# Taking the last pair of chunks of a gated RWKV scan one chunk at a time, with a small part of the last residual on VectorE

## The chip, the cores and the metric

One core of a Trainium2 chip runs the whole program. The metric is device time in microseconds (us), the median over several executions; lower is better. TensorE (PE in the profile) does matrix products into PSUM, VectorE (DVE) and ScalarE (ACT) work on SBUF and PSUM, GpSimd (POOL) works on SBUF only, and SyncE (SP) issues the transfers of this kernel (ACT issues one).

## The reference

The input x has 32 sequences of 128 tokens and 256 channels, in float32. Two residual blocks follow each other:

```python
def _birwkv(r, k, v, w, u):
    ew, ek = jnp.exp(w.reshape(-1)), jnp.exp(k)
    Af, Bf = _wkv_scan(ek, v, ew)                    # forward scan
    Ab, Bb = _wkv_scan(ek[:, ::-1], v[:, ::-1], ew)  # backward scan
    cur = jnp.exp(u.reshape(-1) + k)
    wkv = (Af + Ab[:, ::-1] + cur * v) / (Bf + Bb[:, ::-1] + cur)
    return jax.nn.sigmoid(r) * wkv

x = x + jnp.tanh(g_xattn[0]) * _birwkv(_layernorm(x), ctx, ctx, w, u)
x = x + jnp.tanh(g_ffn[0]) * _L0_ffn_ref(_layernorm(x), ...)
```

The second block quantises its input, the weights (256 to 704 and back) and the hidden values to 8-bit steps. The step of the input comes from the largest absolute value of the whole normalised tensor, so nothing of that block's products can start before all 32 sequences have been normalised.

## The kernel before

**Layout.** Tokens lie on the 128 partitions. `x_all` holds x for all sequences, 256 channels each, and is updated in place. The two scans of a channel are one product with a 128x128 matrix of decay weights, so numerator and denominator of a channel for all 32 sequences come from one matmul.

**The scan stage.** The 256 channels are worked through in 32 chunks of 8 channels, and the chunks in 16 pairs (`PAIRS`, index m; chunk j = 2m or 2m + 1). One chunk is 8 x 32 = 256 values in a partition. For a chunk, `accumulate(j)` on TensorE makes 16 matmul pieces (line 909) and gives `ab_done`; `denominator(j)` on VectorE (line 706) multiplies the denominator with 1 + exp(-normalised x) and gives `den_done`; `reciprocal(m)` on ScalarE takes both chunks of a pair at once, a Ln (line 493) and an Exp (line 496) of 512 values, since exp(-ln d) is 1/d, and gives `rden_done`; `mix(j)` on VectorE (line 715) multiplies the numerator with it and gives `mix_done`; `residual(m)` on GpSimd (line 397) adds both chunks of a pair into `x_all` and gives `x1_done`.

**Order around the last pairs.** Each engine runs its own queue in the written order. VectorE does the denominator of a chunk of the next pair ahead of each mix; after pairs 10 to 15 it also runs `early_stats` (line 679), the statistics of the first 128 channels, for six sequences at a time (two after the last pair). ScalarE runs one more weight copy (`keep_weights(2)`), a change of its function table and a tanh after the last reciprocal.

**The normalisation stage.** For eight groups of four sequences, `late_stats(g)` on VectorE waits for all of `x1_done`, takes the statistics of the second 128 channels (line 679) and merges both halves (line 695); `rstd2(g)` on GpSimd is four small operations (lines 365 to 371); `normalise(g)` on ScalarE (line 504) does three sequences of the group and `normalise_last(g)` on GpSimd (line 421) the fourth; `turn_z(g)` on TensorE transposes the result (line 933), `keep_z(g)` on ScalarE copies it out of PSUM (line 511), and `peak_z(g)` on VectorE finds the largest value (line 722). GpSimd runs `rstd2(0)`, then `rstd2(g + 1)` and `normalise_last(g)` in turn. VectorE runs `late_stats` of groups 0 to 2 and then alternates `peak_z(g - 3)` and `late_stats(g)`. From group 3 on TensorE adds five idle products of 512 columns behind each group (`idle_wide`, line 956). ScalarE alternates `normalise(g)` and `keep_z(g - 1)`. Then follow the global peak, the gate and up products (line 1002), the down products (line 1035) and the output.

Of the kernel before, what the change touches and what calls it, by code (L numbers as in the profile page):

```python
# [22 lines left out]
ALU = mybir.AluOpType  # L23
# [17 lines left out]
def gated_rwkv_ffn(nc, x, ctx_kv, g_xattn, g_ffn, w, u, clip_x, clip_down, w_gate, w_up, w_down, out):  # L41
    SEQS, T, C = x.shape
# [22 lines left out]
    BANKS = 6  # L65
    HALF = CK * SEQS
    assert T == P and IR == P // 2 and UNIT == 512 and CH == 2 and 2 * HALF == 512 and CG == 2

    with ExitStack() as stack:
# [111 lines left out]
        def group(tile, g):  # L181
# [34 lines left out]

            "ctx_back", "ek_done", "pk_done", "ab_done", "den_done", "ln_done", "rden_done", "mix_done", "x1_done",

# [112 lines left out]
        def _(pool):  # L331
# [61 lines left out]
            def residual(m):  # L393
# [4 lines left out]
                                        ALU.add).then_inc(s["x1_done"], 1)  # L398

            for g in range(GROUPS):  # L400
                rstd1(g)
# [7 lines left out]
            own_weights(0)  # L409
            for m in range(PAIRS):  # L410
                residual(m)
                j = 2 * (m + 1) + 6
                if j in MADE:
                    add_own(MADE.index(j))
                    if j != MADE[-1]:
                        own_weights(MADE.index(j) + 1)
            def normalise_last(g):

                n = g * GS + GS - 1
                pool.wait_ge(s["sc2_done"], g + 1)  # L420
                nc.gpsimd.tensor_scalar(z_all[:, n * C:(n + 1) * C], x_all[:, n * C:(n + 1) * C], rs2[:, n:n + 1],  # L421
                                        mr2[:, n:n + 1], ALU.mult, ALU.add).then_inc(s["z_last"], 1)
# [34 lines left out]
        def _(act):  # L457
# [31 lines left out]
            def reciprocal(m):  # L489

                act.wait_ge(s["den_done"], 2 * m + 2)
                wait(act, s["rden_done"], m)
                nc.scalar.activation(lnd, den[:, m % 2, :], ACT.Ln).then_inc(s["ln_done"], 1)  # L493
                act.wait_ge(s["ln_done"], m + 1)
                wait(act, s["mix_done"], 2 * m - 2)
                nc.scalar.activation(rden[:, m % 2, :], lnd, ACT.Exp, scale=-1.0).then_inc(s["rden_done"], 1)  # L496

            def normalise(g):
# [79 lines left out]

            for m in range(PAIRS):
                reciprocal(m)  # L580
# [8 lines left out]
                if m == 12:  # L589
                    exp_clips()  # L590
            keep_weights(2)
            tanh_ffn()
# [48 lines left out]
        def _(dve):  # L641
# [45 lines left out]
            def late_stats(g):  # L687

                dve.wait_ge(s["x1_done"], PAIRS)
                for i in range(GS):  # L690
# [19 lines left out]
            def mix(j):  # L710
                m, i = j // 2, j % 2
                dve.wait_ge(s["rden_done"], m + 1)
                if i == 0:
                    wait(dve, s["x1_done"], m - 1)
                nc.vector.scalar_tensor_tensor(mixed[:, m % 2, i * CK:(i + 1) * CK, :], half_bank(j, 1), S["tanh_x"],  # L715
                                               rden[:, m % 2, i * HALF:(i + 1) * HALF].rearrange("p (c b) -> p c b", b=SEQS),
                                               ALU.mult, ALU.mult).then_inc(s["mix_done"], 1)

            def peak_z(g):
# [34 lines left out]
            done = 0  # L754
            for m in range(PAIRS):
                if m + 1 < PAIRS:
                    denominator(2 * m + 2)
                mix(2 * m)
                if m + 1 < PAIRS:
                    denominator(2 * m + 3)  # L760
                mix(2 * m + 1)
# [10 lines left out]
                if m > 9:  # L772
                    n = min(6, SEQS - done)
                    early_stats(done, n)
                    done += n
            assert done == SEQS
            for g in range(GROUPS):
                if g >= 3:
                    peak_z(g - 3)
                late_stats(g)  # L780
            for g in range(GROUPS - 3, GROUPS):
                peak_z(g)
# [283 lines left out]
```

## Time and profile before

| what | value |
|---|---|
| device time, median of 3 runs | 218.35 us (218.22 to 220.37) |
| the profiled execution, its own time | 217.56 us |
| its span in the profile | 215.6 us |
| busy share of the span: PE, DVE, ACT, POOL | 79%, 79%, 72%, 64% |
| granted TensorE clock, mean | 0.93 of full |

No engine is busy throughout: the program is a row of stages with a different limit in each. The change touches the seam between two of them, from about 96 us to about 108 us of the span, where the scan stage ends and the second normalisation begins. What counts there is the order in which things wait for each other, and the chain of waits and the timelines of the single engines show that; the busy shares do not.

### The profile page before, as it was taken

What the parts mean: (1) busy time and instruction counts of PE and PEld (TensorE: products, weight loads), DVE (VectorE), ACT (ScalarE), POOL (GpSimd) and SP (SyncE); (2) the same over time, 40 slices, a digit from 0 to 9 for tenths busy, and PEclk for the clock granted to TensorE, in tenths of its full rate; (3) what the DMA queues carried; (4) which work ended last, traced back from release to release, by engine and by line L of the source; (5) the groups of instructions that cost most, each with busy time, mean ns of one, the idle gap of its engine ahead of it and who ended that gap; (6) DMA issues with size and microseconds to landing.
All of it is one profiled execution on the core that took longest, in us unless ns stands there. A gap on an engine that the chain in (4) does not pass through costs nothing.

```text
span 215.6 us, 3369 instructions
## 1 busy us (share of the span) xinstructions
PE 169.9 (79%) x1121; PEld 122.7 (57%) x1126; DVE 170.5 (79%) x345; ACT 155.7 (72%) x235; POOL 137.4 (64%) x157
## 2 busy tenths in 40 slices
PE   4599977959899999972078888599799924989950
PEld 4456527959899999962056553234243403756620
DVE  0769495537657689997689679997999998999992
ACT  3459698573996996996479978578798844899400
POOL 3364223469399999884688807749887750039991
PEclk9969999999999999999556999999999995899995
DMA  3999999999999996300000000000000000004458
GB/s 98 341 371 348 348 319 292 287 292 298 289 320 252 267 243 177 101 0 2 0 0 0 0 3 2 0 0 0 3 0 0 0 0 0 3 0 146 167 195 273
DMA packets 43327, 29.30 MB, mean 136 GB/s; under 512 B 2224, under 2 KB 43056, under 8 KB 43312
## 3 DMA queue, kind: packets, MB, share of 16 engines
q1 hardware_dynamic: 43168, 28.84, 46.7%
q10 hardware_dynamic: 144, 0.26, 0.3%
q8 instruction: 9, 0.15, 0.3%
q14 instruction: 6, 0.05, 0.1%
HBM read 24.65 MB, written 4.46 MB: 135 GB/s over the span
## 4 chain that ended last, share of the span: by engine, by line
PE 36%; DVE 25%; ACT 14%; DMA 9%; issue 7%; POOL 3%; SPq 1%; DVEq 1%; ACTq 0%
PE ps L909 10%; PE ps L1002 9%; PE ps L1035 8%; DMA hidden<-lag_w 6%; PE ps L893 5%; DVE hidden L799 4%; DMA hidden<-in_ctx 3%; ACT hidden L504 3%; DVE h_space L856 2%; DVE hidden L817 2%; PE ps L940 2%; DVE h_peaks L828 2%; ACT silu_out L623 2%; ACT hidden L575 2%; DVE bn L679 2%
## 5 line engine op out<-in xcount | busy, mean ns | idle before, releaser
L909 PE MATMUL ps<-hidden 128*128 128x128 f32 (+1 forms) x512 | 58.7, 276 | 6.3 <-DMA hidden<-lag_w 3.0
L909 PEld LDWEIGHTS ps<-hidden 128*128 128x128 f32 x512 | 57.8, 192 | 7.6 <-issue 3.3
L397 POOL TENSOR_TENSOR x_all<-x_all,silu_out 128x512 f32<-128x512 f32 x16 | 24.3, 1526 | 8.2 <-DVE silu_out L715 8.2
L828 DVE TENSOR_REDUCE h_peaks<-hidden (+2 forms) x24 | 26.0, 1123 | 2.0 <-POOL hidden L440 1.3
L1035 PE MATMUL ps<-wdT,z_t 128*128 128x256 bf16 (+1 forms) x192 | 25.0, 285 | 2.9 <-ACT z_t L637 2.9
L706 DVE SCALAR_TENSOR_TENSOR h_space<-z_t,ps 128x256 f32<-128x256 f32 x32 | 18.9, 595 | 8.9 <-PE ps L909 8.7
L637 ACT ACTIVATE z_t<-h_space 128x1024 bf16<-128x1024 int8 (+3 forms) x12 | 20.1, 1754 | 6.8 <-DVE h_space L856 6.8
L1035 PEld LDWEIGHTS ps<-wdT,z_t 128*128 128x128 bf16 (+1 forms) x192 | 17.0, 101 | 10.8 <-issue 4.8
L623 ACT ACTIVATE silu_out<-ps,mix_scale 128x1024 f32<-128x1024 f32 (+1 forms) x18 | 18.3, 1019 | 5.8 <-PE ps L1002 3.4
L933 PE MATMUL ps<-ident,hidden 128*128 128x128 f32 x64 | 11.6, 342 | 12.6 <-POOL hidden L421 11.1
L453 POOL TENSOR_TENSOR x_all<-x_all,z_t 128x512 f32<-128x512 f32 x6 | 10.7, 1802 | 15.5 <-DVE z_t L874 15.5
L715 DVE SCALAR_TENSOR_TENSOR silu_out<-ps,small,silu_out 128x256 f32<-128x256 f32 x32 | 15.2, 477 | 5.7 <-ACT silu_out L496 4.8
L485 ACT ACTIVATE z_t<-x_all,mr,nr 128x256 f32<-128x256 f32 x32 | 16.4, 589 | 3.6 <-POOL mr L359 3.6
L893 PE MATMUL ps<-hidden,flip 128*128 128x512 f32 x32 | 16.1, 646 | 2.8 <-DMA hidden<-in_ctx 2.8
L933 PEld LDWEIGHTS ps<-ident,hidden 128*128 128x128 f32 x64 | 9.6, 179 | 15.4 <-ACT hidden L504 14.5
L440 POOL TENSOR_TENSOR hidden<-silu_out,up_out 128x1024 f32<-128x1024 f32 x6 | 14.5, 2410 | 5.5 <-ACT up_out L627 5.4
L671 DVE BATCH_NORM_STATS2 bn<-x_all 128x6 f32<-128x256 f32 x32 | 11.2, 414 | 8.1 <-DMA x_all<-in_x 7.9
L440 POOL TENSOR_TENSOR hidden<-h_space 128x1024 f32<-128x1024 f32 x6 | 14.4, 2401 | 4.8 <-ACT h_space L627 4.8
L493 ACT ACTIVATE up_out<-h_space 128x512 f32<-128x512 f32 x16 | 10.0, 624 | 10.3 <-DVE h_space L706 10.3
L856 DVE TENSOR_SCALAR h_space<-hidden,small 128x1024 int8<-128x1024 f32 (+3 forms) x12 | 15.2, 1334 | 0.1
L504 ACT ACTIVATE hidden<-x_all,mr,rs 128x256 f32<-128x256 f32 x24 | 12.6, 594 | 3.3 <-POOL mr L371 3.3
L354 POOL TENSOR_TENSOR ve<-mv,consts 128x4 f32<-128x4 f32 x8 | 1.6, 199 | 20.5 <-DVE mv L675 20.5
(105 smaller groups left out, 357.2 us busy)
## 6 DMA issues: line engine op xcount, KB each, us to landing
hidden<-lag_w SPq DMA_DIRECT2D x26, 512.0 KB, 7.3
x_all<-in_x SPq DMA_DIRECT2D x8, 512.0 KB, 8.8
hidden<-in_ctx SPq DMA_DIRECT2D x8, 512.0 KB, 9.0
out<-x_all SPq DMA_DIRECT2D x16, 256.0 KB, 2.4
xq<-in_L_ffn_w_down SPq DMA_DIRECT2D x1, 704.0 KB, 5.9
xq<-in_L_ffn_w_gate SPq DMA_DIRECT2D x1, 640.0 KB, 6.9
h_space<-in_L_ffn_w_up SPq DMA_DIRECT2D x1, 640.0 KB, 6.0
lag_w<-up_out ACTq DMA_DIRECT2D x1, 255.0 KB, 7.2
```

Of the source, the lines that this page charges most:

```text
L397: nc.gpsimd.tensor_tensor(xs, xs, mixed[:, m % 2, :, :].rearrange("p c b -> p b c"), ALU.add).then_inc(s["x1_done"], 1)
L440: nc.gpsimd.tensor_tensor(hidden[:, b * HB + k * BT:b * HB + (k + 1) * BT], silu_even[n % 2], up_even[n % 2], ALU.mult).then_inc(s["h_even ...
L504: last = nc.scalar.activation(z_all[:, n * C:(n + 1) * C], xs[:, i, :], ACT.Identity, scale=rs2[:, n:n + 1], bias=mr2[:, n:n + 1])
L623: nc.scalar.activation(silu_out[:, 1, 0:cols] if k % 2 else silu_even[even % 2], banks[0], ACT.Silu, scale=mix_scale[:, 0, k:k + 1]).then_ ...
L637: nc.scalar.activation(hq[:, b % 2, cols], h8[:, b % 2, cols], ACT.Copy).then_inc(s["hq_done"], 1)
L828: nc.vector.tensor_reduce(h_peaks[:, bass.ds(KA * b + k, 1)], hidden[:, bass.ds(b * HB + k * BT, cols)], AX.X, ALU.max, apply_absolute_val ...
L856: nc.vector.tensor_scalar(h8[:, b % 2, k * BT:last], hidden[:, b * HB + k * BT:b * HB + last], S["inv_h"], None, ALU.mult).then_inc(s["h8_ ...
L893: last = nc.tensor.matmul(turned(g)[:, half], flip[:, :], ring[g % SLOTS][:, half], start=True, stop=True)
L909: last = nc.tensor.matmul(ps[:, j % BANKS, c * 2 * SEQS:end * 2 * SEQS], lag_tile(j)[:, c, :], ekp[:, (j * CK + c) * 2 * SEQS:(j * CK + en ...
L933: last = nc.tensor.transpose(ps[:, z_bank(g) + h, i * T:(i + 1) * T], z_all[:, n * C + h * P:n * C + (h + 1) * P], ident[:, :])
L1002: last = nc.tensor.matmul(dst, wT[:, h, k * P:k * P + rows_], whole_x(b)[:, j, h, :], start=(h == 0), stop=(h == CH - 1))
L1035: last = nc.tensor.matmul(ps[:, 4 * sl + i, j * C:(j + 1) * C], lhs, rhs, start=(k == 0 and j == 0), stop=(k == KA - 1), skip_group_check= ...
```

## The change

- The last pair (chunks 30 and 31) is taken chunk by chunk on ScalarE: a Ln and an Exp of 256 values for each chunk (`reciprocal_half`), with semaphores of their own.
- On VectorE the last steps are put in another order: both mixes of pair 14 stand ahead of the denominator of chunk 31; the mix of chunk 30 stands ahead of it too. The eight early statistics that are left are spread: one, then five, then the last two behind the late statistics of group 0.
- The residual of the last pair is split in three. GpSimd adds chunk 30 for all sequences and chunk 31 for sequences 8 to 31 (`residual_half`); VectorE adds chunk 31 for sequences 0 to 7 (`residual_own`).
- The late statistics of groups 0 and 1 wait for the residual of chunk 30 and for VectorE's own part; those of the later groups wait for everything on GpSimd (each group also behind VectorE's own part by order).

```diff
@@ gpsimd @@
+            def residual_half(j, first):
+
+                pool.wait_ge(s["mix_done"], j + 1)
+                xs = x_all[:, :].rearrange("p (b c) -> p b c", c=C)[:, first:SEQS, j * CK:(j + 1) * CK]
+                part = mixed[:, j // 2 % 2, j % 2 * CK:(j % 2 + 1) * CK, first:SEQS]
+                nc.gpsimd.tensor_tensor(xs, xs, part.rearrange("p c b -> p b c"), ALU.add).then_inc(s["x1_done"], 1)
...
-            for m in range(PAIRS):
+            for m in range(PAIRS - 1):
                 residual(m)
...
+            residual_half(CHUNKS - 2, 0)
+            residual_half(CHUNKS - 1, OWN_SEQS)
@@ scalar @@
+            def reciprocal_half(j):
+
+                m, i = j // 2, j % 2
+                cols = slice(i * HALF, (i + 1) * HALF)
+                act.wait_ge(s["den_done"], j + 1)
+                act.wait_ge(s["rden_done"], m)
+                nc.scalar.activation(lnd[:, cols], den[:, m % 2, cols], ACT.Ln).then_inc(s["ln_half"], 1)
+                act.wait_ge(s["ln_half"], i + 1)
+                act.wait_ge(s["mix_done"], 2 * m - 2)
+                nc.scalar.activation(rden[:, m % 2, cols], lnd[:, cols], ACT.Exp, scale=-1.0).then_inc(s["rden_half"], 1)
...
-            for m in range(PAIRS):
+            for m in range(PAIRS - 1):
                 reciprocal(m)
...
+            for j in (CHUNKS - 2, CHUNKS - 1):
+                reciprocal_half(j)
             keep_weights(2)
@@ vector @@
             def late_stats(g):
 
-                dve.wait_ge(s["x1_done"], PAIRS)
+                if (g + 1) * GS <= OWN_SEQS:
+                    dve.wait_ge(s["x1_done"], PAIRS)
+                    dve.wait_ge(s["x1_own"], 1)
+                else:
+                    dve.wait_ge(s["x1_done"], PAIRS + 1)
...
-                dve.wait_ge(s["rden_done"], m + 1)
+                if m < PAIRS - 1:
+                    dve.wait_ge(s["rden_done"], m + 1)
+                else:
+                    dve.wait_ge(s["rden_half"], i + 1)
...
+            def residual_own():
+
+                j = CHUNKS - 1
+                dve.wait_ge(s["mix_done"], CHUNKS)
+                xs = x_all[:, :].rearrange("p (b c) -> p b c", c=C)[:, 0:OWN_SEQS, j * CK:(j + 1) * CK]
+                part = mixed[:, j // 2 % 2, j % 2 * CK:(j % 2 + 1) * CK, 0:OWN_SEQS]
+                nc.vector.tensor_tensor(xs, xs, part.rearrange("p c b -> p b c"), ALU.add).then_inc(s["x1_own"], 1)
...
+            denominator(CHUNKS - 2)
+            mix(CHUNKS - 4)
+            mix(CHUNKS - 3)
+            early_stats(done, 1)
+            mix(CHUNKS - 2)
+            denominator(CHUNKS - 1)
+            early_stats(done + 1, 5)
+            mix(CHUNKS - 1)
+            residual_own()
             for g in range(GROUPS):
                 if g >= 3:
                     peak_z(g - 3)
                 late_stats(g)
+                if g == 0:
+                    early_stats(SEQS - 2, 2)
```

VectorE's queue before the change, from the denominator of chunk 30 to the first merge of the second normalisation. L706 is the denominator, L715 the mix, L679 the statistics, L695 the merge; `h_space` holds the denominators, `silu_out` the mixed values and the reciprocals:

```order
L706 SCALAR_TENSOR_TENSOR h_space<-z_t,ps 128x256 [waits ln_done,ab_done]
L715 SCALAR_TENSOR_TENSOR silu_out<-ps,small,silu_out 128x256 [waits x1_done,rden_done]
L706 SCALAR_TENSOR_TENSOR h_space<-z_t,ps 128x256 [waits ab_done]
L715 SCALAR_TENSOR_TENSOR silu_out<-ps,small,silu_out 128x256 [waits rden_done]
L679 BN_STATS bn<-x_all 128x6 [waits x1_done]
L679 BN_STATS bn<-x_all 128x6 x5
L715 SCALAR_TENSOR_TENSOR silu_out<-ps,small,silu_out 128x256 [waits x1_done,rden_done]
L715 SCALAR_TENSOR_TENSOR silu_out<-ps,small,silu_out 128x256 [waits rden_done]
L679 BN_STATS bn<-x_all 128x6 [waits x1_done]
L679 BN_STATS bn<-x_all 128x6
L679 BN_STATS bn<-x_all 128x6 [waits x1_done]
L679 BN_STATS bn<-x_all 128x6 x3
```

The same stretch of VectorE's queue after the change (L735 is now the denominator, L747 the mix, L704 the statistics, L757 VectorE's own part of the residual):

```order
L735 SCALAR_TENSOR_TENSOR h_space<-z_t,ps 128x256 [waits ln_done,ab_done]
L747 SCALAR_TENSOR_TENSOR silu_out<-ps,small,silu_out 128x256 [waits x1_done,rden_done]
L747 SCALAR_TENSOR_TENSOR silu_out<-ps,small,silu_out 128x256 [waits rden_done]
L704 BN_STATS bn<-x_all 128x6 [waits x1_done]
L747 SCALAR_TENSOR_TENSOR silu_out<-ps,small,silu_out 128x256 [waits x1_done,rden_half]
L735 SCALAR_TENSOR_TENSOR h_space<-z_t,ps 128x256 [waits ab_done]
L704 BN_STATS bn<-x_all 128x6 [waits x1_done]
L704 BN_STATS bn<-x_all 128x6 x4
L747 SCALAR_TENSOR_TENSOR silu_out<-ps,small,silu_out 128x256 [waits rden_half]
L757 TENSOR_TENSOR x_all<-x_all,silu_out 128x8x8 [waits mix_done]
L704 BN_STATS bn<-x_all 128x6 [waits x1_own,x1_done]
L704 BN_STATS bn<-x_all 128x6 x3
```

The denominator of chunk 31 has moved behind three mixes, only the mix of chunk 31 is left behind it, and an addition of 8 x 8 values stands between that mix and the late statistics.

GpSimd's queue at the same place, before (L397 is the residual, L365 the first operation of `rstd2(0)`):

```order
L397 TENSOR_TENSOR x_all<-x_all,silu_out 128x32x16 [waits mix_done] x4
L365 TENSOR_TENSOR ve<-mv,consts 128x4 [waits mv2_done]
L367 TENSOR_TENSOR rs<-ve,consts 128x4 [waits ve2_done]
L369 TENSOR_TENSOR nr<-rs,consts 128x4 [waits rs2_done]
L371 TENSOR_TENSOR mr<-nr,mv 128x4 [waits rs2_done]
```

and after:

```order
L399 TENSOR_TENSOR x_all<-x_all,silu_out 128x32x16 [waits mix_done] x3
L407 TENSOR_TENSOR x_all<-x_all,silu_out 128x32x8 [waits mix_done]
L407 TENSOR_TENSOR x_all<-x_all,silu_out 128x24x8 [waits mix_done]
L367 TENSOR_TENSOR ve<-mv,consts 128x4 [waits mv2_done]
L369 TENSOR_TENSOR rs<-ve,consts 128x4 [waits ve2_done]
L371 TENSOR_TENSOR nr<-rs,consts 128x4 [waits rs2_done]
L373 TENSOR_TENSOR mr<-nr,mv 128x4 [waits rs2_done]
```

The last addition of 512 values has become one of 256 and one of 192.

## Rows read from the trace of the kernel before

**Rows 1.** The chain of waits, at the seam: start us, length us, what.

```profile
100.67 0.79 DVE silu_out L715 x2
...
101.53 1.50 POOL x_all L397
...
103.05 0.88 DVE bn L679 x4
...
113.81 1.96 PE ps L933 x8
...
115.79 1.02 ACT z_t L511
...
118.28 0.91 ACT z_t L511
```

**Rows 2.** Timeline of DVE: start, length, line, operation [idle before <- releaser].

```profile
96.38 0.59 DVE L706 SCALAR_TENSOR_TENSOR h_space<-z_t,ps 128x256 f32<-128x256 f32 x1
97.02 0.48 DVE L715 SCALAR_TENSOR_TENSOR silu_out<-ps,small,silu_out 128x256 f32<-128x256 f32 x1
98.53 0.58 DVE L706 SCALAR_TENSOR_TENSOR h_space<-z_t,ps 128x256 f32<-128x256 f32 x1 [1.02 <-PE ps L909]
99.03 0.48 DVE L715 SCALAR_TENSOR_TENSOR silu_out<-ps,small,silu_out 128x256 f32<-128x256 f32 x1
99.42 1.25 DVE L679 BATCH_NORM_STATS2 bn<-x_all 128x6 f32<-128x128 f32 x6
100.58 0.86 DVE L715 SCALAR_TENSOR_TENSOR silu_out<-ps,small,silu_out 128x256 f32<-128x256 f32 x2
...
103.05 0.87 DVE L679 BATCH_NORM_STATS2 bn<-x_all 128x6 f32<-128x128 f32 x4 [1.21 <-POOL x_all L397]
```

**Rows 3.** Timeline of DVE further on: the merge of group 1, the first peak.

```profile
105.15 0.42 DVE L695 BATCH_NORM_AGGREGATE mv<-bn 128x2 f32<-128x12 f32 x4
...
108.75 1.22 DVE L722 TENSOR_REDUCE peaks<-hidden 128x1 f32<-128x1024 f32 x1 [1.98 <-POOL hidden L421]
```

**Rows 4.** Timeline of ACT: two Exp of 512, the first operation of the normalisation.

```profile
96.36 0.63 ACT L496 ACTIVATE silu_out<-up_out 128x512 f32<-128x512 f32 x1
...
99.81 0.63 ACT L496 ACTIVATE silu_out<-up_out 128x512 f32<-128x512 f32 x1
...
106.35 1.58 ACT L504 ACTIVATE hidden<-x_all,mr,rs 128x256 f32<-128x256 f32 x3 [3.06 <-POOL mr L371]
```

**Rows 5.** Timeline of POOL: residual of pair 14, first operations of groups 0 and 1.

```profile
99.58 1.50 POOL L397 TENSOR_TENSOR x_all<-x_all,silu_out 128x512 f32<-128x512 f32 x1 [3.46 <-DVE silu_out L715]
...
104.46 0.20 POOL L365 TENSOR_TENSOR ve<-mv,consts 128x4 f32<-128x4 f32 x1 [1.45 <-DVE mv L695]
...
106.27 0.20 POOL L365 TENSOR_TENSOR ve<-mv,consts 128x4 f32<-128x4 f32 x1
```

**Rows 6.** Groups by line and shape: busy us, mean ns | idle before, releaser.

```profile
L564 ACT ACTIVATE xq<-xq 128x256 f32<-128x256 f32 x1 | 0.4, 401 | 0.0
...
L751 DVE TENSOR_SCALAR down_row<-down_row 128x128 f32<-128x128 f32 x1 | 0.2, 227 | 4.1 <-ACT down_row L562 4.1
...
L861 DVE TENSOR_TENSOR small<-small 128x1 f32<-128x1 f32 x1 | 0.2, 157 | 0.0
```

**Rows 7.** Timeline of all engines from 79 us: a DVE operation beside a POOL residual.

```profile
79.21 3.02 POOL L397 TENSOR_TENSOR x_all<-x_all,silu_out 128x512 f32<-128x512 f32 x2
...
80.90 2.65 DVE L735 TENSOR_SCALAR down_diag<-ident,small 128x128 f32<-128x128 f32 x2
```

**Rows 8.** By stretch: PE, PEld, DVE, ACT, POOL busy (count), PEclk, DMA share, GB/s.

```profile
103.50:104.00 0.50, 0.00 (x0) 0.00 (x0) 0.47 (x4) 0.00 (x0) 0.00 (x0) 0.50 0.00 0
...
117.50:118.00 0.50, 0.45 (x4) 0.26 (x3) 0.50 (x4) 0.50 (x2) 0.34 (x3) 1.00 0.00 0
```

**Rows 9.** Timeline of PE: transposes, idle products and transposes at the full clock.

```profile
118.78 1.07 PE L933 MATMUL ps<-ident,hidden 128*128 128x128 f32 x8
119.68 1.24 PE L956 MATMUL ps<-wgT,ident_b 128*128 128x512 bf16 x5
```

More of the change, by code:

```diff
@@ L66, in gated_rwkv_ffn @@
     HALF = CK * SEQS
+    OWN_SEQS = 8
     assert T == P and IR == P // 2 and UNIT == 512 and CH == 2 and 2 * HALF == 512 and CG == 2
@@ L215, in gated_rwkv_ffn @@
             "w_rec", "w_quant", "w_cast", "w_turned", "w_stored",
-            "ctx_back", "ek_done", "pk_done", "ab_done", "den_done", "ln_done", "rden_done", "mix_done", "x1_done",
+            "ctx_back", "ek_done", "pk_done", "ab_done", "den_done", "ln_done", "rden_done", "ln_half", "rden_half", "mix_done", "x1_done", "x1_own",
             "bn1_done", "mv1_done", "ve1_done", "rs1_done", "sc1_done",  "ez_done",
@@ L754, in _ @@
             done = 0
-            for m in range(PAIRS):
-                if m + 1 < PAIRS:
-                    denominator(2 * m + 2)
+            for m in range(PAIRS - 2):
+                denominator(2 * m + 2)
                 mix(2 * m)
-                if m + 1 < PAIRS:
-                    denominator(2 * m + 3)
+                denominator(2 * m + 3)
                 mix(2 * m + 1)
@@ L772, in _ @@
                 if m > 9:
[L773 to L776, printed above, removed]
+                    early_stats(done, 6)
+                    done += 6
+            denominator(CHUNKS - 2)
[7 more added lines that the diff above has]
+            residual_own()
             for g in range(GROUPS):
```

## The prediction

> **What bounds the kernel now.** The busy shares say little here: the four engines lie between 64% and 79%, so the limit changes from stage to stage. I read the chain of waits first, at the seam between the scans and the second normalisation, then the timeline of each engine there.
>
> The chain of waits [rows 1] runs through the last two mixes on DVE (100.67 to 101.46), then through one residual of 1.50 us on POOL (101.53 to 103.03), then into the first late statistics on DVE (103.05). From there it goes on as statistics, small operations on POOL, transposes, and ScalarE's alternating copies and normalisations. DVE's timeline [rows 2] shows both sides of this: it stands idle for 1.21 us before 103.05, released by that POOL residual. Earlier it stands idle for 1.02 us before 98.53, released by PE, whose product for chunk 31 is done only then. So the last denominator cannot start before 98.53, and everything between 98.53 and 103.05, 4.52 us, is what this change can work on. It is made of: the denominator (0.58), Ln and Exp of 512 values on ACT (the second is the row at 99.81, 0.63, ending at 100.44) [rows 4], six early statistics that keep DVE until 100.58 [rows 2], two mixes, and the POOL residual of two chunks.
>
> **What is behind the seam.** All of the second normalisation hangs on the first late statistics. ACT stands idle for 3.06 us before its first normalisation at 106.35 [rows 4], so its work before (a weight copy, the table change, a tanh) is over at 103.29. The stage can come up to 3.06 us earlier before ACT itself refuses. PE has nothing to do between chunk 31 and the first transpose. If the first late statistics start earlier by d, the whole of the rest moves by d, unless something named below stands in the way. No transfer stands at the seam: the outputs are issued at the end.
>
> **The change, step by step.**
>
> *1. PE.* Nothing changes ahead of 98.53. The denominator of chunk 30 (96.38) and the first mix of pair 14 (97.02) stand where they stood [rows 2].
>
> *2. The order on DVE.* A mix lets the next instruction in after 0.39 us (99.03 to 99.42), a denominator after 0.50 (98.53 to 99.03), and six statistics take 1.16 of the queue (99.42 to 100.58), 0.19 each [rows 2]. So: mix 28 at 97.02 as before, mix 29 at 97.41 (before: 99.03), one statistic at 97.80, ready for mix 30 at about 98.0. This fills the 1.02 us in which DVE waited for PE.
>
> *3. ACT, chunk 30.* The Exp of pair 14 ends at 96.36 + 0.63 = 96.99 [rows 4], and the denominator of chunk 30 at 96.97 [rows 2]. An ACT operation of 256 values in SBUF with a constant scale took 401 ns, against 0.63 us for 512 [rows 4, 6]. The old pair took from 99.11 (end of the denominator) to 100.44, that is 1.33 = 2 x 0.63 + 0.07 for the handovers. A half takes 2 x 0.40 + 0.07 = 0.87. So the half for chunk 30 is done at 96.99 + 0.87 = 97.86 and mix 30 runs from 98.0; the queue is free at 98.39, 0.14 before PE releases the denominator of chunk 31. This work is hidden by the wait for PE. If a half cost as much as a whole (1.33), mix 30 would start at 98.35, the denominator would come at 98.74, and 0.2 would be lost.
>
> *4. The path.* Denominator of chunk 31 from 98.53 to 99.11; ACT's half 0.87, until 99.98; meanwhile DVE does five statistics from 99.03, 0.97 us, until 100.00. Mix 31 from 100.01 to 100.49 (0.48 [rows 2]). Before, it ended at 100.58 + 0.86 = 101.44. That is 0.95 us, from the halves on ACT (0.46), the overrun of the sixth statistic (100.58 against 100.44, 0.14) and one mix fewer (0.86 - 0.48 = 0.38), less a handover of 0.03.
>
> *5. The residual.* DVE adds 64 values itself. The trace has no such addition: from below, one value in 0.157; from above, 128 values of one source in 0.227 [rows 6]. I take 0.2. A handover on one engine or from ACT to DVE is 0.03 (96.99 to 97.02 [rows 2, 4]; half of ACT's 0.07): 100.52 to 100.72, and the late statistics of group 0 start at about 100.74. Before, the POOL residual stood there with its handovers: 103.05 - 101.44 = 1.61, now 0.25. That is 1.36.
>
> *6. The other condition.* Group 0 also waits for POOL's part of chunk 30. The residual of pair 14 can start 0.07 behind mix 29 (as 99.58 stood behind 99.51 [rows 2, 5]): 97.41 + 0.48 + 0.07 = 97.96, until 99.46. A residual of 512 values takes 1.50 and a POOL addition of 4 values 0.20 [rows 5], so 2.56 ns for a value: 256 values in 0.85, 192 in 0.68. Chunk 30 is done at about 100.33, 0.2 before DVE wants to start its own. If it took the full 1.5, it would end at 100.97 and cost 0.25 to 0.5.
>
> *7. POOL's part of chunk 31* starts 0.07 behind mix 31, at 100.56, and ends at about 101.25, or 101.45 if it has to let DVE go first. POOL is next wanted at 104.46 - 2.31 = 102.15 for group 0 [rows 5]: covered by 0.7 us. If that cover is gone, every 0.1 of it is 0.1 of the end.
>
> *8. The two statistics left over* (0.39) now stand before group 1. Its merge ended at 105.57 [rows 3]; it now ends at 105.57 - 2.31 + 0.39 = 103.65. POOL took it up at 106.27 [rows 5], which becomes 103.96: hidden by 0.3 us. Group 2 is 0.39 late too, hidden by the 1.98 us in which DVE waits before 108.75 [rows 3]. They cost nothing.
>
> *9. ACT at the other side* is wanted at 106.35 - 2.31 = 104.04 and is free at 103.29 even if it gained nothing. Covered by 0.75.
>
> **Sum.** 0.95 + 1.36 = 2.31 us, the same as 103.05 - 100.74. On the profiled execution: 217.56 - 2.31 = 215.25 (span 213.3). The median of the runs shown is 0.79 above that execution: 218.35 - 2.31 = 216.04. I forecast 216.1.
>
> **A row that speaks against it.** At 79.21 two POOL residuals begin, until 82.23. Two DVE operations of 128 values that fall into them take 2.65 us together, where one like it took 0.227 alone [rows 6, 7]: the first ends behind POOL's work, not beside it. DVE's new addition stands in just such a place. By the Trainium skill (SBUF — State Buffer, "SBUF: two separate sides") GpSimd and VectorE share a pair of ports, a VectorE operation with two SBUF inputs takes that pair, and whoever starts first holds it for its whole instruction. These rows agree with it for a VectorE operation of one input; none of them shows one with two. What decides is the order at 100.5: DVE hears of its own mix after 0.03, POOL after 0.07, so DVE should be first by 0.04 and pay nothing.
>
> **Rivals.**
>
> *A. As summed.* 2.1 to 2.5 us, 215.8 to 216.3. Chance 0.60.
>
> *B. DVE's addition is held by POOL.* Either POOL gets in first with its part of chunk 31: DVE's own is then done 0.68 later, at about 101.45, and the gain is 1.6; or POOL's half for chunk 30 does not shrink with its size and ends at 100.97, gain 1.85. For it: [rows 7], and a margin of only 0.04 and 0.2. Against it: the order of the handovers. 216.5 to 216.8. Chance 0.24.
>
> *C. Nothing is gained at the end.* The seam moves, and a wait further on takes it back, at ACT (cover 0.75), at POOL for group 1 (cover 0.3), or at PE. Against it: each has its cover in steps 7 to 9. About 217.3 to 218.4. Chance 0.11 with partial cases.
>
> *D. Slower: PE comes out of its low clock later.* The clock is at 0.5 (1.2 GHz) from 103.5, 5 us after PE fell idle, and at full (2.4 GHz) at 117.5 [rows 8]; eight transposes take 1.96 at the low level and 1.07 at the high one [rows 1, 9]. ACT's round of one group takes 118.28 - 115.79 = 2.49 [rows 1]. From group 3 PE also does five idle products a group, 1.24 at the high level [rows 9], so about 2.5 at the low: 1.96 + 2.5 = 4.5 against 2.49, 2.0 us late for each group in which the low clock lasts. From two such groups on it is 4.0 against a gain of 2.3: 220.0. Against it: PE's work is the same and only moved, and the rise came with group 3, before the first idle products. A rise that is earlier gains at most 0.25, since ACT has its normalisation to finish before 115.79 anyway. Chance 0.05.
>
> **How the numbers follow.** A change of 1% is 2.2 us, about what a measurement of this kernel can tell from none. The sum is 0.1 above that, so the verdict hangs on small things: A falls on the faster side in somewhat more than two of three cases (0.42), and a little comes from an earlier clock and from noise. Faster by over 1%: 0.45. Within 1%: 0.50 (the rest of A, B, C). Slower: 0.05 (D). The range takes in A and B, a gain larger by up to 0.8 (the median may lie nearer to the profiled execution, 0.79 below it), and part of C: 215.2 to 217.3.
>
> **What the profile after would show.** Mix 31 ends near 100.5; DVE's own addition, of about 0.2 us, follows at once; the late statistics of group 0 start at 100.7 to 100.8 with no wait for POOL; the residual of pair 14 starts at 98.0; POOL's new pieces take 0.85 and 0.68; ACT's first normalisation starts near 104.0 and still has idle time before it; the distance from the first late statistics to ACT's copy of group 3, 118.28 - 103.05 = 15.23 us before [rows 1], is the same. An own addition of 0.7 us or more would be B. A wait of DVE for POOL before group 0 would refute step 6. Five wide idle products of 2.5 us would be D. I would be wrong altogether if the denominator of chunk 31 no longer started at 98.5.

## The result: 0.7% faster, and the profile after

Over 20 runs each the changed kernel took 217.49 us (215.57 to 218.72) and the kernel before 218.65 us (217.42 to 220.53). The ratio is 0.993, with a 95% interval of 0.9907 to 0.9952, so the gain is 1.0 to 2.0 us. I had forecast 216.1 in a range of 215.2 to 217.3, so the direction was right and the median stood just above the range. The range had been laid around the median of three runs (218.35), where twenty gave 218.65; the ratio taken of 218.35 is 216.8, inside the range.

The profiled execution of the changed kernel took 216.45 us, with a span of 214.6 against 215.6. Its chain of waits at the seam (start, length, what), the counterpart of [rows 1]:

```profile
99.60 0.58 DVE h_space L735
100.18 0.97 DVE bn L704 x5
101.15 0.46 DVE silu_out L747
101.61 0.02 issue
101.63 0.28 DVE x_all L757
101.91 0.03 issue
101.94 0.02 DVEq L716
101.96 0.04 issue
102.00 0.88 DVE bn L704 x4
```

The POOL residual of 1.50 us has left the chain. From the start of the denominator of chunk 31 (L735) to the first late statistics it is now 2.40 us, where it was 4.52 [rows 2]: 2.12 us shorter. But the denominator itself starts at 99.60 and not at 98.53, 1.07 later. What releases it, PE's product for chunk 31, was not changed, and its distance from the denominator of chunk 30 is the same (2.16, and 2.15 before), so the delay arises ahead of the changed code. This is why the span is only 1.0 shorter. The prediction had named this very sign, a denominator of chunk 31 that no longer starts at 98.5, as the one by which it would be wrong altogether, and it is what the experiments have to explain.

DVE's timeline, for [rows 2] and [rows 3]:

```profile
97.44 0.59 DVE L735 SCALAR_TENSOR_TENSOR h_space<-z_t,ps 128x256 f32<-128x256 f32 x1
98.09 0.87 DVE L747 SCALAR_TENSOR_TENSOR silu_out<-ps,small,silu_out 128x256 f32<-128x256 f32 x2
98.89 0.28 DVE L704 BATCH_NORM_STATS2 bn<-x_all 128x6 f32<-128x128 f32 x1
99.08 0.47 DVE L747 SCALAR_TENSOR_TENSOR silu_out<-ps,small,silu_out 128x256 f32<-128x256 f32 x1
...
104.49 0.42 DVE L724 BATCH_NORM_AGGREGATE mv<-bn 128x2 f32<-128x12 f32 x4
...
107.69 1.22 DVE L762 TENSOR_REDUCE peaks<-hidden 128x1 f32<-128x1024 f32 x1 [1.59 <-POOL hidden L433]
```

The idle 1.02 us ahead of the last denominator is filled with mix 29, a statistic and mix 30 (mix 28 stood there before). ACT's timeline, for [rows 4]: the halves of chunk 30 and of chunk 31, and the first normalisation:

```profile
98.15 0.42 ACT L516 ACTIVATE up_out<-h_space 128x256 f32<-128x256 f32 x1
98.60 0.42 ACT L519 ACTIVATE silu_out<-up_out 128x256 f32<-128x256 f32 x1
100.22 0.42 ACT L516 ACTIVATE up_out<-h_space 128x256 f32<-128x256 f32 x1 [1.20 <-DVE h_space L735]
100.67 0.42 ACT L519 ACTIVATE silu_out<-up_out 128x256 f32<-128x256 f32 x1
...
105.30 1.58 ACT L527 ACTIVATE hidden<-x_all,mr,rs 128x256 f32<-128x256 f32 x3 [1.37 <-POOL mr L373]
```

POOL's timeline, for [rows 5]: the residual of pair 14, its two pieces of pair 15, the first operations of groups 0 and 1:

```profile
99.05 1.51 POOL L399 TENSOR_TENSOR x_all<-x_all,silu_out 128x512 f32<-128x512 f32 x1 [1.85 <-DVE silu_out L747]
100.52 0.84 POOL L407 TENSOR_TENSOR x_all<-x_all,silu_out 128x256 f32<-128x256 f32 x1
101.68 0.77 POOL L407 TENSOR_TENSOR x_all<-x_all,silu_out 128x192 f32<-128x192 f32 x1 [0.32 <-DVE silu_out L747]
103.41 0.20 POOL L367 TENSOR_TENSOR ve<-mv,consts 128x4 f32<-128x4 f32 x1 [0.97 <-DVE mv L724]
...
105.22 0.20 POOL L367 TENSOR_TENSOR ve<-mv,consts 128x4 f32<-128x4 f32 x1
```

### The profile page after: what moved, and what is told of

Read it like the earlier page. It is cut to its first block, busy times and chain, and to the rows that moved or that the text cites. A ratio compares the mean times of both kernels' runs of the same rounds, so it can differ in the third digit from the quotient of the medians.

```text
span 214.6 us, 3377 instructions
## 1 busy us (share of the span) xinstructions
PE 171.4 (80%) x1121; PEld 124.1 (58%) x1126; DVE 171.0 (80%) x346; ACT 156.1 (73%) x237; POOL 137.6 (64%) x158
## 4 chain that ended last, share of the span: by engine, by line
PE 35%; DVE 22%; ACT 15%; DMA 9%; issue 7%; SPq 6%; POOL 3%; DVEq 1%; ACTq 0%
PE ps L1050 9%; PE ps L1083 9%; PE ps L941 7%; PE ps L957 7%; DMA hidden<-lag_w 6%; DVE hidden L847 4%; DMA hidden<-in_ctx 3%; ACT hidden L527 3%; SPq L273 2%; DVE h_space L904 2%; DVE hidden L865 2%; PE ps L988 2%; DVE h_peaks L876 2%; ACT hidden L598 2%; ACT silu_out L648 2%
## 5 line engine op out<-in xcount | busy, mean ns | idle before, releaser
L957 PE MATMUL ps<-hidden 128*128 128x128 f32 (+1 forms) x512 | 60.6, 280 | 5.7 <-DVE hidden L678 2.5
L957 PEld LDWEIGHTS ps<-hidden 128*128 128x128 f32 x512 | 59.5, 196 | 7.2 <-DMA hidden<-lag_w 5.7
L735 DVE SCALAR_TENSOR_TENSOR h_space<-z_t,ps 128x256 f32<-128x256 f32 x32 | 19.0, 597 | 10.2 <-PE ps L957 10.0
L399 POOL TENSOR_TENSOR x_all<-x_all,silu_out 128x512 f32<-128x512 f32 x15 | 22.8, 1533 | 6.1 <-DVE silu_out L747 6.0
L747 DVE SCALAR_TENSOR_TENSOR silu_out<-ps,small,silu_out 128x256 f32<-128x256 f32 x32 | 15.2, 477 | 4.3 <-ACT silu_out L508 2.6
L505 ACT ACTIVATE up_out<-h_space 128x512 f32<-128x512 f32 x15 | 9.3, 623 | 9.3 <-DVE h_space L735 9.3
L598 ACT ACTIVATE hidden<-down_row,xq 128x128 f32<-128x128 f32 x48 | 14.6, 388 | 0.0
```

The costliest lines, as they stand in the source:

```text
L399: nc.gpsimd.tensor_tensor(xs, xs, mixed[:, m % 2, :, :].rearrange("p c b -> p b c"), ALU.add).then_inc(s["x1_done"], 1)
L735: nc.vector.scalar_tensor_tensor(den[:, m % 2, i * HALF:(i + 1) * HALF].rearrange("p (c b) -> p c b", b=SEQS), ez[:, :, j * CK:(j + 1) * C ...
L957: last = nc.tensor.matmul(ps[:, j % BANKS, c * 2 * SEQS:end * 2 * SEQS], lag_tile(j)[:, c, :], ekp[:, (j * CK + c) * 2 * SEQS:(j * CK + en ...
```

## The experiments

### Both kernels again: what scatters is not the seam

The two kernels unchanged.

> The kernel before, unchanged, profiled again beside the others. The question is where the seam's 2.12 us (4.52 to 2.40 from the start of the denominator of chunk 31 to the first late statistics) went, when the median moved by 1.2 to 1.5. Theory J (jitter ahead of the seam): the start of that denominator scatters by a microsecond or so from execution to execution of one and the same program, through the landing of the decay matrices and through where small VectorE operations meet POOL's; here it starts anywhere from 98 to 100, the seam is 4.5 and the rest from the first late statistics to the end of the span is 112.55 again. Theory S (systematic): the start is 98.5 again within 0.2 and only the changed kernel has it later. Ratio to the kernel before 1.000 under both.

> The changed kernel, unchanged, profiled again. Theory J: seam 2.40, rest 112.6, and a start of the denominator of chunk 31 that differs from the 99.60 of the first profile and may lie as low as 98.5; ratio 0.990 to 0.993. Theory S: the start is 99.6 again within 0.2, ratio 0.993 or above.

> The changed kernel once more, to narrow the ratio: 0.993 [0.9907, 0.9952] and 0.9898 [0.9857, 0.9939] so far. If the 2.12 us of the seam all reach the end, 0.990 is expected over many runs (2.12 of 219); if a part is given back, 0.993. Seam again 2.40, the start of the denominator of chunk 31 anywhere from 98.5 to 100.5.

The kernel before against itself: 1.0016 (0.9983 to 1.0049), with single runs from 217.26 to 221.53. The changed kernel: 0.9898 (0.9857 to 0.9939), median 216.88, and 0.9907 (0.9875 to 0.9939), median 217.05. Two rows of DVE's timeline of the kernel before, profiled again:

```profile
100.30 0.58 DVE L706 SCALAR_TENSOR_TENSOR h_space<-z_t,ps 128x256 f32<-128x256 f32 x1 [1.02 <-PE ps L909]
...
104.82 0.87 DVE L679 BATCH_NORM_STATS2 bn<-x_all 128x6 f32<-128x128 f32 x4 [1.21 <-POOL x_all L397]
```

The same code starts its last denominator at 98.53 in one execution and at 100.30 in the next; the seam is 4.52 in both. So theory J holds in its first part, and theory S, which had the start of the old code at 98.5 each time, falls. A small shift remains possible: in the table below the three profiles of the kernel before start at 99.2 on average and the nine others at 99.6, too few to tell. Theory J's second part missed: the rest behind the first late statistics was not 112.55 again but 114.1 in both kernels' second profiles (114.08 and 114.26). I divide each profile of this study into four stretches: the start of the denominator of chunk 31; from there to the first late statistics (the seam); from there to the search of the overall peak (the normalisation); from there to the end of the span.

| kernel | starts at | seam | normalisation | rest | span |
|---|---|---|---|---|---|
| before | 98.53 | 4.52 | 23.67 | 88.88 | 215.6 |
| before, again | 100.30 | 4.52 | 23.66 | 90.42 | 218.9 |
| changed | 99.60 | 2.40 | 23.66 | 88.94 | 214.6 |
| changed, again | 99.44 | 2.40 | 23.76 | 90.50 | 216.1 |
| changed, third | 99.14 | 2.40 | 23.97 | 90.39 | 215.9 |
| halves only | 99.79 | 3.60 | 24.35 | 90.16 | 217.9 |
| split only | 99.58 | 3.67 | 23.80 | 90.45 | 217.5 |
| own part late | 98.77 | 2.99 | 23.76 | 90.38 | 215.9 |
| DVE adds all of chunk 31 | 100.79 | 2.74 | 23.66 | 88.91 | 216.1 |
| PE kept busy | 99.65 | 2.41 | 24.36 | 90.28 | 216.7 |
| changed, product earlier | 99.84 | 2.40 | 23.66 | 87.80 | 213.7 |
| before, product earlier | 98.75 | 4.52 | 23.98 | 87.75 | 215.0 |

The seam is the same to 0.01 us wherever the code at it is the same. The other stretches scatter. The start does so by 2.3 us over all twelve profiles and by 1.8 within the kernel before (98.53 and 100.30); what makes it scatter was not looked for. The normalisation scatters by 0.7 over all and by 0.3 within the changed kernel. The rest, in the ten profiles without the earlier product, is either 88.9 or 90.2 to 90.5, with nothing between. The kernel before had, in the profile that I predicted from, the earliest start of all and one of the short rests.

### The rest of 88.9 or of 90.4: PE's clock

PE's timeline among the first gate and up products. In the changed kernel's first profile, a short one:

```profile
134.59 1.03 PE L1050 MATMUL ps<-xq,wgT 128*128 128x512 bf16 x4
137.84 1.04 PE L1050 MATMUL ps<-xq,wuT 128*128 128x512 bf16 x4 [2.22 <-DVE hidden L865]
138.71 1.03 PE L1050 MATMUL ps<-xq,wgT 128*128 128x512 bf16 x4
```

and in the kernel before, again, a long one:

```profile
137.41 1.03 PE L1002 MATMUL ps<-xq,wgT 128*128 128x512 bf16 x4
140.66 1.54 PE L1002 MATMUL ps<-xq,wuT 128*128 128x512 bf16 x4 [2.22 <-DVE hidden L817]
142.00 1.91 PE L1002 MATMUL ps<-xq,wgT 128*128 128x512 bf16 x4
143.70 1.41 PE L1002 MATMUL ps<-xq,wuT 128*128 128x512 bf16 x4
```

PE waits 2.22 us for a product on DVE in both. In the second the granted clock is at 0.5 from 141.1 to 144.5, and four products take 1.91 instead of 1.03. The same holds in all ten profiles: in the seven long rests the clock is at 0.5 for 3.4 us behind this wait, in the three short ones it stays at full. The first gate and up products of the next block (at 142.06 and 146.25) come 1.4 us later behind the search of the peak in the long case, nearly the whole difference. To take the wait away, DVE does that product two quantisations earlier:

```diff
             for n in range(2, GROUPS):
                 quantise_x(n)
+                if n == 5:
+                    multiply(0, 1)
...
-                multiply(b, 1)
+                multiply(b, 1) if not first else None
```

> The changed kernel with one edit far behind the seam: VectorE does the first gate-times-up product (hidden tile 1) two quantisations earlier, behind group 5 and not behind group 7. So far the stretch from the search of the overall peak to the end of the span is either 88.9 us or 90.2 to 90.5 in one and the same program; in the long ones PE stands idle for 2.2 us while it waits for that product and comes back at 1.2 GHz for some 3.4 us. Theory G: with the wait of 2.2 us gone the clock does not fall there, and the stretch is 88.9 or less every time; the median is 216.0 or less, ratio to the kernel before 0.985 to 0.988. Rival: VectorE is what limits the stage, the two quantisations that are now later hold POOL's and PE's next block up, and the stretch is 90 or more, ratio 0.991.

> The kernel before with the same edit. If the seam's 2.12 us reach the end in full, the difference between this and the run of the changed kernel with the edit is 2.1 us (1.0%), and the scatter of both is smaller than without it. If a part is given back somewhere, the difference is 1.2 to 1.6 as the first measurement had it. Ratio to the kernel before 0.994 to 0.998 under theory G, 1.000 under the rival.

The changed kernel with the edit: 215.38 us, ratio 0.9827 (0.9783 to 0.9872). The kernel before with it: 217.26, ratio 0.9924 (0.9895 to 0.9953). DVE's product and PE's longest wait at this place, in the changed kernel with the edit:

```profile
133.87 1.28 DVE L862 SCALAR_TENSOR_TENSOR hidden<-ps,mix_scale,silu_out 128x1024 f32<-128x1024 f32 x1 [0.47 <-ACT silu_out L648]
```
```profile
140.33 0.63 PE L1052 MATMUL ps<-xq,wuT 128*64 128x512 bf16 x4 [1.32 <-DVE hidden L862]
```

The wait of 2.22 is gone, another of 1.32 comes some 3 us later, the clock stays at full there in both profiles, and the rest is 87.80 and 87.75: 1.1 below the short case and 2.6 below the long one. Theory G held, with a larger gain than it said. This is the fastest kernel of the study. The difference between the two medians is 217.26 - 215.38 = 1.88 us. That lies between the 2.1 and the 1.2 to 1.6 of the expectation, and 6 and 11 runs do not know it to better than about 1 us.

### One part alone: the halves

The last pair chunk by chunk and DVE's new order, with the residual as before:

```diff
-            residual_half(CHUNKS - 2, 0)
-            residual_half(CHUNKS - 1, OWN_SEQS)
+            residual(PAIRS - 1)
...
+                dve.wait_ge(s["x1_done"], PAIRS)
...
-            residual_own()
```

> One part alone: the last pair chunk by chunk on ScalarE and VectorE's new order, but the residual of the last pair as before, 512 values on POOL, and all groups wait for it. By the chain of waits: mix 31 ends 2.0 after the start of the denominator of chunk 31, then 0.07 + 1.50 + 0.03, so the seam is 3.6 against 4.52 before: 0.9 gained there, ratio 0.9957. The rival, that the halves gain nothing because the residual is what counts: seam 4.5, ratio 1.000.

DVE's timeline, from the denominator of chunk 31:

```profile
99.79 0.58 DVE L730 SCALAR_TENSOR_TENSOR h_space<-z_t,ps 128x256 f32<-128x256 f32 x1
...
101.30 0.48 DVE L742 SCALAR_TENSOR_TENSOR silu_out<-ps,small,silu_out 128x256 f32<-128x256 f32 x1
...
103.39 0.87 DVE L703 BATCH_NORM_STATS2 bn<-x_all 128x6 f32<-128x128 f32 x4 [1.60 <-POOL x_all L399]
```

The seam is 3.60, as expected: this part is worth 0.92. The measured ratio, 0.9982 (0.9941 to 1.0024), is too wide to tell 0.9957 from 1. This profile also has a long normalisation, 24.35. PE's and ACT's rows show why:

```profile
116.44 1.94 PE L975 MATMUL ps<-ident,hidden 128*128 128x128 f32 x8 [0.35 <-issue]
118.60 1.91 PE L998 MATMUL ps<-wgT,ident_b 128*128 128x512 bf16 x4 [0.22 <-issue]
120.30 1.24 PE L975 MATMUL ps<-ident,hidden 128*128 128x128 f32 x8
```
```profile
121.58 1.02 ACT L533 ACTIVATE z_t<-ps 128x1024 f32<-128x1024 f32 x1 [0.58 <-PE ps L975]
```

The clock was still low at the idle products of group 3, they took about twice as long, and ACT waited for the transposes behind them. This is rival D of the prediction, at its smallest: 0.7 us and not several.

There is a milder form, and it occurs in the changed kernel itself. In its third profile the clock rose before the transposes of group 2; PE then stood idle for 1.23 us, and the transposes of group 3 were at the low clock again:

```profile
112.32 1.06 PE L981 MATMUL ps<-ident,hidden 128*128 128x128 f32 x8 [0.80 <-POOL hidden L433]
114.62 1.79 PE L981 MATMUL ps<-ident,hidden 128*128 128x128 f32 x8 [1.23 <-ACT hidden L527]
```
```profile
119.35 1.02 ACT L534 ACTIVATE z_t<-ps 128x1024 f32<-128x1024 f32 x1 [0.41 <-PE ps L981]
```

The twelve profiles fall into three kinds by this. Where the clock rises during the transposes of group 3 or at the first idle products behind them, the normalisation is 23.66 (five profiles, among them both of the kernel before and one of the changed kernel). Where it rises before the transposes of group 2, it is 23.76 to 23.98 (five, among them the changed kernel's other two and the kernel before with the product earlier). Where the first four idle products still take 1.91, it is 24.35 and 24.36 (two).

### The other part alone: the residual in three parts

The residual in three parts and the two leftover statistics behind group 0, but Ln and Exp of the last pair whole and DVE's old order:

```diff
-            mix(CHUNKS - 3)
-            early_stats(done, 1)
-            mix(CHUNKS - 2)
             denominator(CHUNKS - 1)
-            early_stats(done + 1, 5)
+            mix(CHUNKS - 3)
+            early_stats(done, 6)
+            mix(CHUNKS - 2)
             mix(CHUNKS - 1)
```

> The other part alone: Ln and Exp of the last pair whole and VectorE's order as before up to mix 31 (six early statistics ahead of mix 30), but the residual in three parts as in the changed kernel, the two leftover statistics behind group 0. POOL's residual of pair 14 ends 2.55 after the denominator of chunk 31 starts, its part of chunk 30 takes 0.85, so this and no longer VectorE's own part lets group 0 start, at 3.45: a gain of 1.1 at the seam, ratio 0.995. If the parts were independent (1.36 as in the sum) the seam would be 3.16, ratio 0.9938. VectorE's own part meets POOL's part of chunk 30 here: if the two share a port and the later waits, it takes 0.3 to 0.6 instead of 0.27.

The timeline of all engines at the seam:

```profile
102.18 1.51 POOL L407 TENSOR_TENSOR x_all<-x_all,silu_out 128x256 f32<-128x256 f32 x2
102.52 0.62 DVE L752 TENSOR_TENSOR x_all<-x_all,silu_out 128x64 f32<-128x64 f32 x1
...
103.25 0.49 DVE L702 BATCH_NORM_STATS2 bn<-x_all 128x6 f32<-128x128 f32 x2
```

POOL is working on chunk 30 when DVE's own part is issued at 102.52; that part takes 0.62 instead of 0.27, and the seam is 3.67, not 3.45. (The last row of this view, and of the next such view, shows only the two of the four statistics that lie in its window.) This part alone is worth 0.85. Together with the halves' 0.92 that makes 1.77, less than the 2.12 of both by the 0.35 that the own part is stretched here: the new order lets POOL begin pair 14 0.55 ahead of the denominator of chunk 31 (99.05 against 99.60) where it begins 1.05 behind it here (100.63 against 99.58), so that its piece is out of the way when DVE adds its own. The ratio, 0.9997 (0.9956 to 1.0037), again cannot tell.

### DVE's own part behind POOL's start

```diff
             mix(CHUNKS - 1)
+            early_stats(SEQS - 2, 2)
             residual_own()
...
-                if g == 0:
-                    early_stats(SEQS - 2, 2)
```

> The changed kernel with the two leftover statistics (0.39 us) between mix 31 and VectorE's own part of the residual, so that POOL starts its 192 values first. Theory L (the one that comes first keeps the other out until it is done): VectorE's own part shows 0.27 plus what is left of POOL's 0.7, it ends with or just behind POOL's part, some 0.85 to 0.95 behind mix 31 instead of 0.3, and the seam is 3.0 to 3.1; ratio to the kernel before 0.993. Rival (they only share the width or do not meet): the own part still takes 0.27 to 0.35, ends 0.75 behind mix 31, seam 2.79 to 2.85, ratio 0.992.

The timeline of all engines:

```profile
100.85 0.68 POOL L407 TENSOR_TENSOR x_all<-x_all,silu_out 128x192 f32<-128x192 f32 x1 [0.33 <-DVE silu_out L747]
101.08 0.58 DVE L757 TENSOR_TENSOR x_all<-x_all,silu_out 128x64 f32<-128x64 f32 x1
...
101.76 0.49 DVE L704 BATCH_NORM_STATS2 bn<-x_all 128x6 f32<-128x128 f32 x2
```

Theory L held. With POOL first, POOL's part takes 0.68 and DVE's is stretched to 0.58, ending at 101.66, 0.13 behind POOL's end. With DVE first, as in the changed kernel, DVE's takes 0.27 and POOL's 0.77. The seam is 2.99; ratio 0.994 (0.9905 to 0.9975). The Trainium skill (SBUF — State Buffer, "SBUF: two separate sides") says that whichever of a GpSimd operation and a VectorE operation with two SBUF inputs starts first holds the shared pair of ports for its whole instruction and blocks the other fully. The trace agrees where POOL is first. Where DVE is first, POOL's piece grows only from 0.68 to 0.77, though 0.22 of DVE's addition was still to run when it began, so a full block is not seen in that direction.

### DVE adds chunk 31 for all sequences

```diff
-    OWN_SEQS = 8
+    OWN_SEQS = 32
...
-            residual_half(CHUNKS - 1, OWN_SEQS)
```

> VectorE adds chunk 31 for all 32 sequences, 256 values, and POOL only chunk 30. By the row of 64 values at 0.27, with about 1 ns for each further value, 0.47: the seam is 2.60, 0.2 longer than in the changed kernel, ratio 0.991. If POOL's part of chunk 31 had slowed anything behind the seam (the statistics, group 1), this would show as a rest shorter by that; I expect none. If a two-input addition of this size is slower than that row says (1.5 us as beside POOL in the tail), the seam is 3.6.

DVE's timeline:

```profile
102.83 0.60 DVE L756 TENSOR_TENSOR x_all<-x_all,silu_out 128x256 f32<-128x256 f32 x1
103.53 0.87 DVE L703 BATCH_NORM_STATS2 bn<-x_all 128x6 f32<-128x128 f32 x4
```

256 values take 0.60 and not 0.47: 0.33 for 192 more, 1.7 ns each. The seam is 2.74, 0.34 more than with eight sequences, and nothing behind it got shorter (normalisation 23.66). Ratio 0.9945 (0.9916 to 0.9974). So at the seam it pays that DVE takes only what the first two groups need; the ratios of the two (0.9907 for the changed kernel beside it) are too close to tell.

### PE kept busy between the stages

```diff
+            pe.wait_ge(s["mix_done"], CHUNKS - 2)
+            idle_wide(34)
```

> The changed kernel with 34 idle products of 512 columns on PE behind the product of chunk 31 (7.3 us at the high clock), as soon as mix 29 has freed bank 5, so that PE does not fall idle between the scans and the first transpose. In the prediction I said that an early rise of the clock is worth at most 0.25. Theory: the eight transposes of groups 0 to 2 take 1.07 instead of 1.95 and ScalarE's copies follow earlier; from the first late statistics to ScalarE's copy of group 2 0.25 less (my claim) or 0.9 less (if each group's copy lets the next normalisation go earlier). Seam unchanged at 2.40; ratio to the kernel before 0.989 or 0.986. Rival: the products delay the first transpose, and the rest is longer.

PE's timeline:

```profile
99.66 7.29 PE L1004 MATMUL ps<-wgT,ident_b 128*128 128x512 bf16 x33
107.82 1.06 PE L981 MATMUL ps<-ident,hidden 128*128 128x128 f32 x8 [0.87 <-POOL hidden L433]
110.12 1.06 PE L981 MATMUL ps<-ident,hidden 128*128 128x128 f32 x8 [1.23 <-issue]
112.85 1.94 PE L981 MATMUL ps<-ident,hidden 128*128 128x128 f32 x8 [1.67 <-POOL hidden L433]
```

This missed. Groups 0 and 1 were transposed at the full clock, but they leave gaps of 1.2 and 1.7 us, and by group 2, the one that ACT waits for, the clock was low. It came back too late for group 4, and the normalisation was 24.36. Ratio 0.993 (0.990 to 0.9961), no better than without. What the high clock is worth at group 2 can be read elsewhere: ACT's copy of that group starts 12.74 behind the first late statistics in the changed kernel's first profile and 12.51 and 12.50 in its two others, where PE was at the full clock for it. That is 0.24, my 0.25. It was lost again: in those two profiles the clock was low at group 3 (the milder form above), and the whole normalisation was 0.10 and 0.31 longer than in the first.

## Why the prediction was right, point by point, and where it was off

**The mechanism (case A)** was right. DVE no longer waits for POOL, and the seam got shorter by 2.12 in every profile (2.11 in the one with added idle products), against a sum of 2.31. The sign by which the prediction would have been wrong altogether, a start of the last denominator other than 98.5, did appear, but it appeared in the old code as well (100.30), so it was a bad sign: it took the start of one execution for a property of the kernel.

**Steps 2 and 3.** Right: mixes 28, 29 and 30 and one statistic fit ahead of the denominator of chunk 31. An ACT operation of 256 values took 0.42 (0.40 assumed), the half of a pair 0.87.

**Step 4.** Mix 31 ends 1.99 behind the start of the denominator (1.96 by the sum; 2.91 before). The gain here is 0.92 instead of 0.95, which the halves alone showed.

**Step 5** is the term that was mis-sized: from the end of mix 31 to the first late statistics 0.41, where I had 0.25. DVE's own part took 0.27 instead of 0.2, and the late statistics started 0.10 behind it instead of 0.03; the chain shows DVE's queue between them (101.94), where two semaphores are now waited for in turn. This is 1.20 instead of 1.36 gained.

**Steps 6 and 7.** POOL's pieces took 0.84 and, undisturbed, 0.68, as worked out from 512 and 4 values (0.85 and 0.68). Chunk 30 was done 0.27 before DVE's own part began, chunk 31 0.96 before POOL was wanted.

**Steps 8 and 9.** Right: group 1's merge ended at 104.91, POOL took it up at 105.22; ACT still waited 1.37 before its first normalisation, and DVE 1.59 before the first peak. The distance from the first late statistics to ACT's copy of group 3, by the chain of waits, was 15.23 in the first profile, the same as before. So rival C did not occur there.

**Rival B** did not occur in the changed kernel, and the mechanism behind it is real: where POOL was let in first, the seam was 0.59 longer: DVE's own part began 0.27 later behind mix 31 (0.31 instead of 0.04), and took 0.31 longer (0.58 instead of 0.27). With nothing in between it could hardly have ended sooner, since it ended just behind POOL's piece; so the loss would be about the same 0.6 (an estimate, not run), where the prediction had 0.7. DVE's own part took 0.27 in all five profiles with this code at the seam: it was always first, by 0.04 to 0.05, as the handovers had it. Of the row that spoke against it, [rows 7], only the first DVE operation falls into the two residuals and ends 0.09 behind them (82.32); the second, from 82.4, stands beside the next POOL operation (82.18 to 83.46) and ends 0.09 behind that. Both fit the same reading.

**Rival D** was mispriced. A low clock at the idle products of group 3 costs 0.7, not 2.0 and more, since it ended during them; it is seen once in the halves-only profile, and once where idle products were added ahead. And a clock that rises earlier was to gain at most 0.25: it did gain 0.24 at group 2, and then cost 0.10 to 0.32 at the end, because it fell again for group 3.

**From the sum to the medians** the prediction was weakest. It took the path of one execution for that of the median: "if the first late statistics start earlier by d, the whole of the rest moves by d" is true of stretches, but start, normalisation and rest scatter from execution to execution: within one and the same program by up to 1.8, 0.3 and 1.6 us. The profile before had the earliest start and the shortest form of the other two. Against 20 runs of the kernel before (218.65), 2.12 would give 216.5; the three series gave 217.49, 216.88 and 217.05. Weighted by their intervals the three ratios make 0.992, give or take 0.002: 1.8 us, 1.4 to 2.2. With the product earlier in both kernels it is 1.88. So 2.12 lies at the edge of what was measured. Whether 0.2 to 0.3 of it is given back somewhere in the median, through the clock's behaviour in the later stretches, or whether this is sampling, stays open. The profiles show losses of that size (the 0.10 and 0.31 of the normalisation in two of three profiles of the changed kernel), but the old kernel with the earlier product has one too (0.32), so they cannot be laid to the change. The chance of 0.50 for "within 1%" was earned by the closeness of the sum to 1%, not by the scatter, which I had not seen.

## What to carry to other kernels

Where two stages meet, find the last operation that the second one waits for and ask how little of it its first step needs: give exactly that to the engine that already holds the data, and let the rest follow behind. Before you believe a change of 1%, profile the old kernel twice: stretches that differ between two executions of the same code tell how far medians can be trusted, and the seam itself can then be read to a hundredth of a microsecond where the total cannot. A wait of 2 us of the matrix engine can be followed by a low clock that costs another 1.5 us, so ask what else can fill it.

## What the runs showed of the hardware that I had not expected

- A VectorE addition of two SBUF inputs that is issued while POOL adds is stretched until just behind POOL's end: 0.62 and 0.58 instead of 0.27 for 64 values.
- The same wait of 2.22 us of PE is followed by the full clock (2.4 GHz) in some executions of one program and by 1.2 GHz for 3.4 us in others, and this makes 1.4 of the 1.5 us between a short and a long rest. In the two profiles without the wait the clock did not fall there, and the rest was shorter by 1.1 and 2.6 us.
- Keeping PE busy for 7.3 us ahead of a row of short transposes with gaps of 1.2 and 1.7 us only moved the time at which the clock fell: groups 0 and 1 took 1.06 each, group 2 1.94.
- A clock that rose one group earlier was no gain: the transposes of that group took 1.06 instead of 1.94, PE stood idle for 1.2 us behind them instead of 0.35, and the clock was low again for the next group.
- The addition of 8 x 32 values with rows of 8 costs DVE 1.7 ns for each further value (0.60 for 256 values, 0.27 for 64).
